# Last four pairs of a four-layer attention kernel in half sets, and the scan begun between them

## The reference

```
layer 0: x = x + self_attention_16_heads(layer_norm(x), mask) + memory @ Wg;  x = x + relu(layer_norm(x) @ W1) @ W2
layer 1: one-head attention of layer_norm(x) over layer_norm(ctx), a gelu of width 4, a second one-head attention, skips
layer 2: 16-head causal attention, queries from x, keys and values from ctx; layer norm; gelu(x @ W1) @ W2
layer 3: 8-head attention, queries from layer_norm(x), keys and values from layer_norm(ctx); then
         U = (layer_norm(x) @ W_in.T + b_in) @ Bmat
         s_t = silu(s_(t-1) @ A.T) + u_t          for the 128 tokens t, one after the other, states of 64 numbers
         out = x + states @ Cmat + mean(program_probs) @ W_prog.T + b_prog
```

## Time and profile before

| | |
|---|---|
| three runs, us | 791.69, 793.87, 795.31 (median 793.87) |
| profiled execution: span from first to last instruction, us | 789.9 |
| its own time | the page gives no other than the span; the median run has 4.0 us more than that |
| busy share of the span | PE 95%, DVE 72%, ACT 55%, POOL 43% |
| granted TensorE clock, mean | 0.993 |
| engines on the chain that ended last | PE 70%, DVE 14% |

### The profile page before, as it was taken

How to read it: one execution, slowest core, us unless ns; L and a number is a source line. 1 busy time by engine, 2 the same in 40 slices (tenths; PEclk the granted TensorE clock), 3 DMA queues, 4 the chain that set the end, 5 groups by cost and what they waited for, 6 DMA issues and landing times.

```text
span 789.9 us, 17323 instructions
## 1 busy us (share of the span) xinstructions
...
## 2 busy tenths in 40 slices
PE   6799989999999999998999999999999979989997
...
PEclk9999999999999999999999999999999999999999
...
DMA packets 17897, 22.33 MB, mean 28 GB/s; under 512 B 4109, under 2 KB 14482, under 8 KB 17170
## 3 DMA queue, kind: packets, MB, share of 16 engines
...
...
## 4 chain that ended last, share of the span: by engine, by line
PE 70%; DVE 14%; issue 4%; SPq 4%; ACT 3%; POOL 3%; DMA 0%; DVEq 0%; POOLq 0%
PE work_bank L659 21%; PE work_bank L668 16%; PE work_bank L922 6%; PE scores_bank L707 3%; PE scores_bank L831 3%; PE work_bank L651 3%; PE work_bank L742 3%; DVE probsT L1242 3%; PE work_bank L629 2%; DVE probs L1137 2%; ACT probs L1375 2%; DVE xn L1155 2%; SPq L556 2%; PE work_bank L786 1%; SPq L528 1%
## 5 line engine op out<-in xcount | busy, mean ns | idle before, releaser
L1004 POOL TENSOR_TENSOR probs<-probs,rtotal 128x512 f32<-128x512 f32 (+1 forms) x164 | 165.9, 1025 | 208.1 <-DVE rtotal L1231 207.9
L1375 ACT ACTIVATE probs<-probs,nmx 128x128 f32<-128x128 f32 x512 | 198.0, 390 | 72.5 <-DVE nmx L1137 72.1
L1242 DVE COPY probsT<-work_bank 128x512 f32<-128x512 f32 (+1 forms) x164 | 106.4, 664 | 17.1 <-PE work_bank L922 16.8
L668 PE MATMUL work_bank<-L_w,hidden 128*128 128x256 f32 x512 | 113.6, 380 | 0.0
L668 PEld LDWEIGHTS work_bank<-L_w,hidden 128*128 128x128 f32 x512 | 96.1, 190 | 12.8 <-ACT hidden L1427 0.2
L922 PE MATMUL work_bank<-ident,probs 128*128 128x128 f32 x640 | 92.5, 279 | 5.2 <-POOL probs L1004 3.6
L1375 ACT ACTIVATION_READ_ACCUMULATOR probs<-probs,nmx 128x1 f32 x512 | 96.5, 189 | 0.0
L922 PEld LDWEIGHTS work_bank<-ident,probs 128*128 128x128 f32 x640 | 72.3, 142 | 24.4 <-POOL probs L1004 11.0
L1004 POOL TENSOR_TENSOR rstd<-veps,half 128x2 f32<-128x2 f32 (+1 forms) x59 | 40.6, 687 | 116.0 <-DVE veps L1188 115.8
L1137 DVE CUSTOM_DVE_ANT_0 probs<-scores_bank,bias 128x128 f32<-128x128 f32 x256 | 56.8, 283 | 10.9 <-PE scores_bank L707 10.7
L659 PE MATMUL work_bank<-B_actT,L_w 128*128 128x256 f32 (+1 forms) x288 | 60.7, 359 | 1.0 <-DVE B_actT L1205 1.0
...
## 6 DMA issues: line engine op xcount, KB each, us to landing
...
```

The lines of the kernel that those rows point to most:

```text
L668: mm = nc.tensor.matmul(d[:, b * D:b * D + D], xT, w, start=(n == 0), stop=(n == len(todo) - 1))
L1004: return nc.gpsimd.tensor_tensor(out, a0, a1, op)
L1242: nc.vector.tensor_copy(turn_slot(s, i, key)[:, 0:n], d[:, 0:n * P].rearrange("p (j k) -> p j k", j=n))\
L1375: ins = nc.scalar.activation(e_at[slot][:, j, :], src, ACT.Exp, bias=nmx[:, slot, j:j + 1], scale=1.0 if s == "C" else -1.0, accum_out=tot ...
```

## The change

Pairs 4 to 7 are now all split for layers 2 and 3 (FULL = 4): units 4 to 7 are their tokens 0 to 63, units 8 to 11 tokens 64 to 127. The first scan step comes when units 0 to 7 have their `drive`; steps 2 to 60 are entries of their own in the orders of three engines, between the products of units 8 to 11. All four hand-written orders and LOAD_ORDER are new throughout.

In steps 1 to 60 (EARLY) Silu is made of Tanh: ACT computes tanh(z/2) into `bent`, DVE multiplies (bent + 1) by z in the bank, which gives twice the silu; the next matmul takes A halved (`a_half`). From step 61 on it is ACT's Silu again. The scan lives in work bank 3 up to step 63, so from the first step on the other fills take turns in three banks (BANK_OF, USE_OF).

Keys and values of pairs 4 to 7 need homes of their own (`keys_2`, `values_2`, `keys_3`, `values_3`): they take weights and tiles of layer 0 that are no longer read. A new GpSimd step `zero` clears the padding of two of them. The output of layer 1 goes straight into `x7_all` (tile x4 is gone), for split pairs by four additions on DVE instead of one (L1284, L1289). `exp` of a half unit of layer 2 comes in two entries of two tiles (`expp`, `exp`), its `ffn2` in four of four matmuls (`ffn2p`, `ffn2`). OCCUPIED keeps only its three entries of the start; between steps 2 and 60 there are no unread matmuls. The final stage has 24 products of `last_part` instead of 32, 32 SBUF-to-SBUF moves ahead of the stores instead of 4 + 24.

The core of the diff (of the two `step` entries near its end the first is VectorE's, the second ScalarE's):

```diff
+FULL = 4
+def halved(s, i):
+    return s in "BC" and i >= FULL
+
 def blocks(s, i):
-    return (i - (NT - 1),) if s in "BC" and i >= NT - 1 else tuple(range(PAIR))
+    return ((i - FULL) % 2,) if halved(s, i) else tuple(range(PAIR))
...
 def keys_pair(i):
-    return min(i, NT - 1)
+    return i if i < NT else i - NT + FULL
...
+EARLY = sum(x[0] == "S" for x in program("d"))
+BANK_OF = [n % W_BANKS if n < FILLS_BEFORE_SCAN else (n - FILLS_BEFORE_SCAN) % (W_BANKS - 1) for n in range(len(FILLS))]
...
-STEPS_BEFORE = {("C", 8, ("turn", 2)): 3, ("C", 8, ("turn", 3)): 2, ("C", 8, ("mix",)): 4, ("C", 8, ("out",)): 2,
-            ("C", 8, ("flip", "x7")): 7, ("C", 8, ("drive",)): 3}
...
+            def start_scan():
+                ready(drained[W_BANKS - 1], USES[W_BANKS - 1])
+                for at in emptied_last([("C", j, ("drive",)) for j in range(NT)]):
+                    ready(*at)
+                from_u(0).then_inc(stepped, 1)
+
+            def scan_step(t):
+                pe.wait_ge(silued, t - 1)
+                if t == 32 and t // 32 <= EARLY // 32:
+                    from_u(1)
+                nc.tensor.matmul(scan_bank(t)[0:SS, (t % 32) * B:(t % 32) * B + B], (a_half if t - 1 <= EARLY else a_t)[:],
+                                 w_state[:, t - 1, :], start=False, stop=True, skip_group_check=True).then_inc(stepped, 1)
...
+                elif kind == "step":
+                    dve.wait_ge(bent_at, key)
+                    nc.vector.scalar_tensor_tensor(w_state[:, key, :], bent[:], 1.0, w_bank[W_BANKS - 1][0:SS, at:at + B],
+                                                   ALU.add, ALU.mult).then_inc(silued, 1)
...
+                elif kind == "step":
+                    act.wait_ge(stepped, key)
+                    nc.scalar.activation(bent[:], w_bank[W_BANKS - 1][0:SS, at:at + B], ACT.Tanh, scale=0.5).then_inc(bent_at, 1)
...
-            act.wait_ge(*filled_at("C", NT - 1, "out"))
-            nc.scalar.activation(w_state[:, 0, :], zero[:], ACT.Silu)
-            for t in range(1, P):
+            nc.scalar.activation(w_state[:, P - 1, :], zero[:], ACT.Silu)
+            for t in range(EARLY + 1, P):
```

More of the change, by code:

```diff
@@ L43 @@
 TENSOR_ORDER = """
[L44 to L88, removed]
@@ L89 @@
[L89 to L91 removed]
+H0.flip.x G0.flip.cn H0.k H0.v H0.q J0.k A0.score.0 J0.v K0.k K0.v A0.score.1 H1.flip.x G0.fold A0.turn.0 A0.turn.3
+A0.turn.1 A0.turn.2 A0.turn.5 H1.k A0.mix.0 A0.turn.6 A0.turn.4 A0.turn.7 A0.mix.1 H1.v A0.out.1 A0.out.0 H1.q
@@ new lines @@
+A6.rec.4 M4.turn.s A6.turn.5 C3.flip.x6 A6.turn.1 A6.max.7 M4.self A6.turn.0 A6.rec.7 A6.max.6 A5.ffn1.2 A6.turn.4
+C3.max.3 C3.max.0 A6.rec.6 C3.max.1 C3.max.2 C3.rec.3 A6.mix.0 C3.rec.0 C3.rec.2 C3.rec.1 A5.ffn2 M5.stat.x3
+A6.turn.7 A6.turn.6 C3.turn.0 C3.turn.1 B4.max.3 C3.turn.2 C3.turn.3 A6.mix.1 B4.max.2 B4.rec.3 H7.v C3.mix
+M5.norm.x3 B4.max.0 B4.rec.2 B4.max.1 M5.flip.x3 B4.rec.0 G6.stat.c C3.out C3.stat.x7 G6.norm.c B4.rec.1 A6.out.0
+C3.norm.x7 M5.max.a A6.out.1 M5.rec.a A6.stat.x2 C3.flip.x7 B4.turn.2 A6.norm.x2 B4.turn.3 B4.turn.0 C3.drive
@@ new lines @@
+C7.flip.x6 B9.max.0 B10.rec.2 B10.turn.3 B10.turn.0 B9.max.3 B9.rec.1 B9.max.2 B10.turn.1 B9.rec.0 B10.turn.2
+B9.turn.1 C7.max.1 B9.rec.3 C7.max.0 B10.mix.0 B9.turn.0 C7.rec.0 C7.max.2 B10.flip.o B9.rec.2 C7.max.3 B10.stat.x5
+C7.rec.2 B9.turn.3 C7.rec.3 C7.turn.0 B10.norm.x5 C7.rec.1 B9.turn.2 C8.max.0 C8.max.2 C8.max.1 B10.flip.x5
+C7.turn.1 B9.mix.0 C8.max.3 C7.turn.3 C7.turn.2 B9.flip.o C8.rec.0 B9.stat.x5 C8.rec.3 C8.rec.1 C8.rec.2 C7.mix
+B9.norm.x5 C7.out B9.flip.x5 C7.stat.x7 C8.turn.0 C8.turn.1 C7.norm.x7 C7.flip.x7 C8.turn.3 C7.drive S0.step.1
```

672 lines of the change are left out of this document (397 added, 275 removed), and 4 rows, old and new, of the table OCCUPIED.

## The result

The changed kernel takes 812.72 us (median of 4 runs, 809.9 to 814.88), the kernel before 792.78 (789.29 to 795.31) on the same chip: a ratio of 1.0256, 95% interval 1.0216 to 1.0297. It is slower by 20 us where I had forecast 771 and a gain. The profiled execution's own time is 814.88, its span 813.1; of the four it is the longest.

What follows compares the result with a forecast made beforehand. TensorE's work was taken to bound the kernel up to `M7.self`, then gaps and a serial scan chain; 541.9 + 48 + 62 + 71 + 44.8 = 767.7 us of span, 771 of time, a gain of 2.9%, range 760 to 782.

Steps and rivals of the forecast that it cites:

- Step 60 to the end: Last 67 scan steps: 44.8 us (43.8 to 47), against 43.8 before, mainly for Silu's table load.
- rival B: Stage after `M7.self` stays as sparse as before: 81 us in place of 62, time 790; chance 0.13.
- Up to `A7.ffn2`: Start to `A7.ffn2`: 38 us less from moved work and 3 won at the start, mark at 541.9.
- `A7.ffn2` to `M7.self`: Stage between these marks: nearly the same products as before, 48 us again (46 to 52).
- `M7.self` to the first step: Stage before the scan: 51.7 us of products, 62 us taken between bounds 55 and 81, since extra halves wait for nothing.
- The 60 steps: Scan steps laid among products: largest engine sum per gap gives 67 us, 71 taken, upper end 85; a bare step 0.82.
- Rival A: Steps queue behind everything in three in-order queues: region 107 us, time 808, slower; chance 0.10.
- Rival C: Tanh is not in Gelu's table: nine table loads in place of three, 8 us more, 779; chance 0.17.
- The sum: Five stages give 767.7 us of span against 789.9; with 4.0 for the median run 771.7, said as 771.
- The chances: Forecast 0.60; over all cases faster 0.81, same 0.10, slower 0.09.

Runs made afterwards that it cites:

- before_bare: The kernel before, without its 41 unread matmuls between steps 24 and 66 of the scan: 817.03 us, ratio 1.03 to the kernel before.
- hold_all: `hold_wide_rows` plus nineteen unread matmuls in three stalls (ahead of `B1.turn.6`, `C6.mix`, `B8.flip.x5`): 781.42 us, ratio to before 0.9864.
- hold_two: The changed kernel plus two unread matmuls in each bare gap between steps, one in every other gap from step 45: 805.82 us, ratio to before 1.0131.
- hold_wide: `hold_two` with 384 columns in the unread matmuls behind steps 61, 62, 65 and 66: 799.51 us, ratio to before 1.0091.
- hold_wide_rows: `hold_wide` with the split pairs' last products as one 256-column matmul and an unread one, for two of 128: 785.42 us, ratio to before 0.9921.
- raise_rows: The changed kernel plus wide unread matmuls behind steps 61, 62, 65, 66 (three behind 61) and 256-column last products of split pairs: 789.26 us, ratio to before 0.9966.
- steps_last: `hold_all` with all `step` entries behind `C11.drive`, one unread matmul ahead of each product, two behind each step: 892.38 us, ratio to before 1.1251.
- dips_only: The changed kernel plus only the nineteen unread matmuls in three stalls, nothing in the region of steps: 808.73 us, ratio to before 1.0206.

## Why the prediction was wrong

**The step that failed** is *Step 60 to the end*: "43.8 us before, for the same 67 steps", and 44.8 with what is new. It was 71.6. I carried the old step's period into a place whose clock I hadn't asked about. The clock at each stage stood in the earlier trace rows, as 0.99 to 1.00 but for one stage at 0.95; I had read that the unread matmuls between steps 2 and 60 go, and used it only in rival B, for another stage. `before_bare` shows that thinning of this kind alone is worth 24 us. In `hold_all`, with the same last steps and three banks but a full clock, this stretch takes 47.9, so the rival that the experiments began with, the stretch's own structure, is out for all but 3.1 of the 26.8 us. These 3.1 are about what three terms give that I did not have: the two u products, which now stand behind step 60 and which I overlooked there (0.98 for 0.55 each, 0.9), the four wide matmuls (three at 0.98, one at 0.79, 1.5), and the split pairs' products with their unread ones (0.7 for 0.58 on average, 1.0), 3.4 together; the last two are the price of the mends. By `hold_two`, `hold_wide` and `hold_wide_rows` there are three thinned places: the bare steps, the two u products, the split pairs' last products; `raise_rows` shows that the first may fall if a burst follows. The first and the last stood in my text as edits, the second not at all, and none with its effect on the clock.

The Trainium skill (TensorE: Matmul & The Clock Gate, Part 1) says that "the default state is throttled, and activity releases the throttle". The runs agree in part: where the work was thinned the clock was lost (717.6), but in `steps_last` two unread matmuls a step, with TensorE shown busy without a gap for 78 us, did not release it. None of the numbers above rests on the page.

**Up to `A7.ffn2`**: 551.3 for 541.9. The stretch at half clock near 209 is 2.9 to 5.3 of that, by `hold_all` (548.4) and `dips_only` (546.0). The other 4 to 6.5 us are at the size I had given the density of a new order; what causes them was not looked into and stays open.

**`A7.ffn2` to `M7.self`**: 45.7 for 48, just under my 46 to 52, with the clock full.

**`M7.self` to the first step**: 72.6 for 62; the clock is 2.1 of the difference (70.5 in `hold_all`). The rest, 8.5, is a term mis-sized: I chose the dense end of 55 to 81. At full clock TensorE is busy 61.9 of 69.6 us and VectorE 55.2, in stage cuts that `hold_all` shows above. What I had counted as 51.7 us of products shows as 62 busy, tails and, in `hold_all`, 12 unread matmuls included, so 62 left no room for any wait. Rival B was half right in the time (81 for 62); of its reasons the clock gave 2.1 us, and the shared tiles were not tested.

**The 60 steps**: 71.8 for 71 is luck: the last 24 us of them ran at half clock, of which nothing was in my sum. At full clock (`hold_all`) they take 66.9, where the sum of the largest in each gap was 67. The method held, and the 4 us that I added for imperfect overlap were not needed; a bare step is 0.76 where I had 0.82. Rival A (107) is out. `steps_last` adds the estimate that without the steps the region would be at most 10 us shorter. None of the eight norms there was slowed (0.41 each, not the 1.27 of the earlier trace rows), and the step's operation took 0.16.

**Rival C**, at 0.17 the likeliest, is out. ScalarE's table loads in the region of the changed kernel, from the groups of instructions (busy us, mean ns, idle before):

```profile
L1489 ACT ACT_TABLE_LOAD x1 | 1.3, 1283 | 0.0
L1553 ACT ACT_TABLE_LOAD x1 | 1.3, 1283 | 0.0
L1496 ACT ACT_TABLE_LOAD x1 | 1.3, 1283 | 0.0
```

Three, as in the forecast, not nine: Tanh needs no load beside Gelu, nor beside Exp. The Trainium skill (ScalarE: Activation LUTs, What ACT_TABLE_LOAD costs) prices a switch at 2.66 us, 1.28 of it the load and the rest a drain. The load here is 1.28 too, but the next operation begins 1.30 us after the load does; the drain does not show.

**The sum**: 767.7 + 9.4 - 2.3 + 10.6 + 0.8 + 26.8 = 813.0 of span. With the clock kept, `hold_all`: 767.7 + 6.5 - 2.2 + 8.5 - 4.1 + 3.1 = 779.5 of span, 781.4 of time. So with its clock kept the change gains 1.4% (10 to 11 us), half of the 2.9% forecast; the clock and what thinned it account for the 31 us between `hold_all` and the changed kernel. The 4.0 us between span and time was wrong too: it set a median run beside another execution's span, and a run's time is 1.8 above its own span (814.88 and 813.1; 791.69 and 789.9 before). Whether the kernel before would gain from the same care was not tried; its clock was at half for some 10 us in all.

**The chances** gave slower 0.09. No rival had the clock in the last stretch, though two of the three rivals that I did write ended near or above 790. The way of the change, slower, came by none of the mechanisms that I had priced.
